# Two-layer cross-attention: the last 64 key columns computed by token beside the values, then turned by two transposes

## The reference, cut to what matters

```python
# layer 0: tokens 0..76 are text, 77..255 are image tokens
q = split_heads(x @ Wq.T); k = split_heads(text @ Wk.T); v = split_heads(text @ Wv.T)
k_ip = split_heads(ip @ Wk_ip.T); v_ip = split_heads(ip @ Wv_ip.T)
out = merge(attend(q, k, v)) + merge(attend(q, k_ip, v_ip))
x = out @ Wo.T + bo + x
# layer 1: tokens 0..251 are text, the last 4 image tokens
probs_t = softmax(q @ k_t.T / 4); text_out = probs_t @ v_t
qsem = l2norm(probs_t @ text); sem = qsem @ l2norm(ip).T
probs_ip = softmax(q @ k_ip.T / 4 + 0.5 * sem) * spatial_mask
x = merge(text_out + probs_ip @ v_ip) @ W_out + b_out + x
```

## Time and profile before

| what | value |
|---|---|
| median of three runs | 808.55 us |
| the profiled execution's own time | 811.3 us |
| its span, first to last instruction | 809.5 us |
| TensorE (PE) busy | 771.5 us, 95% |
| VectorE (DVE) busy | 562.1 us, 69% |
| ScalarE (ACT) busy | 426.0 us, 53% |
| GpSimd (POOL) busy | 402.2 us, 50% |
| mean granted TensorE clock | 0.992 |

### The profile page before, as it was taken

The page is one execution under the profiler, slowest core; times in us unless marked ns, Lnnn a source line. Parts: engine busy times, 40 slices in busy tenths (PEclk is TensorE's granted clock), DMA queues, the critical chain, the costliest instruction groups (busy, mean ns, idle before and its releaser), DMA issues.

```text
span 809.5 us, 17185 instructions
## 1 busy us (share of the span) xinstructions
PE 771.5 (95%) x6360; PEld 626.8 (77%) x6360; DVE 562.1 (69%) x1533; ACT 426.0 (53%) x913; POOL 402.2 (50%) x297
## 2 busy tenths in 40 slices
PE   5989899999999999999999999999999999988796
PEld 4888688888888878887877788788887887766474
DVE  4366465757576666758769778688697787686854
ACT  5234546463646474646465565555554655455551
POOL 5511222020202040405568877788769768779663
PEclk9999999999999999999999999999999999999998
DMA  7875835665647472736263355153172441400010
GB/s 245 212 210 157 212 112 135 197 159 158 162 126 184 126 202 76 211 99 170 70 150 94 90 143 151 45 160 112 49 190 69 111 126 62 113 1 26 12 33 17
DMA packets 103027, 100.67 MB, mean 124 GB/s; under 512 B 10264, under 2 KB 102176, under 8 KB 102944
## 3 DMA queue, kind: packets, MB, share of 16 engines
q1 hardware_dynamic: 101408, 98.26, 44.4%
q10 hardware_dynamic: 1536, 1.31, 0.6%
HBM read 61.65 MB, written 36.74 MB: 122 GB/s over the span
## 4 chain that ended last, share of the span: by engine, by line
PE 75%; DVE 9%; issue 4%; DMA 4%; POOL 3%; ACT 3%; SPq 1%; POOLq 0%; DVEq 0%; ACTq 0%
PE pB L384 22%; PE pB L500 12%; PE pB L463 8%; PE pB L486 8%; PE pB L584 5%; PE pPV L527 4%; PE pPV L522 4%; PE pPV L532 4%; PE pB L541 3%; PE pPV L518 3%; POOL Y L1306 2%; DVE m_sb L1061 2%; DVE m_sb L1059 2%; DMA QP<-mlo 1%; DMA Y<-in_Wk 1%
## 5 line engine op out<-in xcount | busy, mean ns | idle before, releaser
L1306 POOL TENSOR_TENSOR Y<-P,wv 128x512 f32<-128x512 f32 x120 | 156.2, 1318 | 107.8 <-ACT P L854 107.7
L1076 DVE TENSOR_TENSOR Y<-pB,Y 128x512 f32<-128x512 f32 x160 | 108.8, 686 | 70.0 <-PE pB L500 60.1
L463 PE MATMUL pB<-KP,QP 96*128 96x256 f32 x640 | 130.2, 288 | 2.7 <-DMA KP<-k0d 1.6
L1283 POOL TENSOR_TENSOR klo<-xin,khi 128x256 fp32r<-128x256 f32 x18 | 13.2, 756 | 228.8 <-ACT khi L765 228.8
L463 PEld LDWEIGHTS pB<-KP,QP 96*128 96x128 f32 x640 | 107.1, 192 | 16.5 <-issue 5.8
L1061 DVE TENSOR_REDUCE m_sb<-pB 128x2 f32<-128x504 f32 x160 | 108.0, 676 | 11.4 <-PE pB L463 9.7
L486 PE MATMUL pB<-QP,KP 100*128 100x512 f32 x320 | 108.3, 418 | 5.1 <-DMA QP<-mlo 4.4
L854 ACT ACTIVATE P<-pB 128x512 f32<-128x512 f32 x160 | 86.5, 597 | 42.0 <-PE pB L486 32.1
L854 ACT ACTIVATE P<-pB,ln 128x512 f32<-128x512 f32 x160 | 101.1, 691 | 0.0
L844 ACT ACTIVATE wv<-pB 128x512 fp32r<-128x512 f32 x120 | 66.8, 591 | 57.0 <-PE pB L486 55.7
L765 ACT ACTIVATE Vs<-pPV 128x512 f32<-128x512 f32 (+1 forms) x80 | 39.4, 492 | 101.8 <-PE pPV L522 68.4
(11 more groups left out here) (180 smaller groups left out, 1701.1 us busy)
## 6 DMA issues: line engine op xcount, KB each, us to landing
QP<-q0d SPq DMA_DIRECT2D x64, 192.0 KB, 4.1
KP<-k0d SPq DMA_DIRECT2D x64, 192.0 KB, 4.3
c_sb<-in_cT SPq DMA_DIRECT2D x16, 512.0 KB, 5.1
q0d<-qhi SPq DMA_DIRECT2D x32, 256.0 KB, 2.5
k0d<-khi SPq DMA_DIRECT2D x30, 256.0 KB, 2.5
q0d<-qlo SPq DMA_DIRECT2D x16, 256.0 KB, 2.8
k0d<-klo SPq DMA_DIRECT2D x15, 256.0 KB, 2.6
VB<-vipd SPq DMA_DIRECT2D x6, 640.0 KB, 4.0
```

The lines of the kernel that those rows point to most:

```text
L463: made = mm(bank[:, sc * S:sc * S + S], QP[i][0:KROWS, j, a, sc * 128:sc * 128 + 128], KP[i][0:KROWS, j, :], start=True, stop=True)
L1076: tt(Y[:, p, dst, :], bank_of["gp", q, dst][:, :], Y[:, p, dst, :], MUL).then_inc(dv_y, 1)
L1306: tt(Y[:, p, ch, :], P[:, p, ch, :], PH[q % HR][ch].bitcast(F32), SUB).then_inc(po_y, 1)
```

## The change

The last 64 key columns are no longer a job of matmuls with the weights stationary. Their weights (`wkz`) stand behind the value weights in one buffer (`wvk`), so that each matmul of V1 and V2 moves 384 columns instead of 320 and gives, by token, the image values and the last 64 image keys. ScalarE copies 128 columns of the result (the 64 keys with 64 value columns ahead of them) into `kz`; the job Kb is now two transposes of 128x128 of `kz`, after V2. Their result has the keys in partitions 64 to 127; the high part is written into `klo[64:128, 2]`, the low part into `klo[0:64, 2]`, a half buffer that the query and x tiles do not share. The third transpose of KT is made 128 wide, so that the text keys land in the same half.

The jobs' order changes with it (V1, V2 ahead of Kb; in layer 0 V0 between them, in layer 1 G0), and so do the pace table and the signals: the stores of `k0d` count on `l_k`, those of `k1d` on `l_kz`, and the load of the third key pack moves from step 9 of slot u to step 1 of slot u+1. In the prologue ScalarE and GpSimd split `wvi` ahead of `wv`, and ScalarE stores `k0d` after V1 and `k1d` after Kb.

```diff
-JOBS = (("Qa", "Qb", "Kt", "Ka", "Kb", "KT", "V0", "V1", "V2"),
-        ("Qa", "Qb", "Ka", "Kb", "V1", "V2", "G0", "G1"))
-SIZE = {"Qa": 16, "Qb": 8, "Kt": 12, "KT": 3, "Ka": 24, "Kb": 12, "V0": 12, "V1": 12, "V2": 12, "G0": 12, "G1": 12}
-PACE = ((14, 14, 13, 12, 12, 11, 10, 10, 9, 6), (13, 13, 12, 12, 12, 11, 11, 10, 8, 6))
-FIRST = (9, 9, 9, 9, 9, 9, 9, 9, 9, 30)
+JOBS = (("Qa", "Qb", "Kt", "Ka", "KT", "V1", "V2", "V0", "Kb"),
+        ("Qa", "Qb", "Ka", "V1", "V2", "G0", "Kb", "G1"))
+VALUES = ("V0", "V2")
+SIZE = {"Qa": 16, "Qb": 8, "Kt": 12, "KT": 3, "Ka": 24, "Kb": 2, "V0": 12, "V1": 12, "V2": 12, "G0": 12, "G1": 12}
+PACE = ((13, 12, 12, 11, 10, 10, 9, 9, 8, 7), (12, 12, 11, 11, 11, 10, 10, 9, 7, 5))
+FIRST = (8, 8, 8, 8, 8, 8, 8, 8, 8, 29)
...
-        wki = sb("wki", [128, 2, EC, C], F32R)
-        wvi = sb("wvi", [128, 2, EC, C], F32R)
+        wkm = sb("wkm", [128, 2, EC, 256], F32R)
+        wvk = sb("wvk", [128, 2, EC, C + 64], F32R)
+        wvi, wkz = wvk[:, :, :, 0:C], wvk[:, :, :, C:C + 64]
+        kz = sb("kz", [128, 2, 128])
...
+                    elif job == "Kb":
+                        pe.wait_ge(ac_bg, job_no(u, "V2"))
+                        for ch in range(2):
+                            made = nc.tensor.transpose(bank[:, 128 * ch:128 * ch + 128], kz[:, ch, :], ident[:, :])
...
+                        ts = slice(0, 128) if job == "V1" else slice(128, S)
+                        yield from chain(bank[:, 0:C + 64], [(c, v) for v, c in pairs512(wvk, slice(0, C + 64), ts)], pe_bg)
...
+                    if job != "V0":
+                        if u:
+                            ac.wait_ge(pe_bg, job_no(u - 1, "Kb"))
+                        copy(kz[:, int(job[1]) - 1, :], bank[:, C - 64:C + 64])
...
+                elif job == "Kb":
+                    ac.wait_ge(l_kz, 48 * u)
+                    if L == 0:
+                        copy(klo[64:128, 2, TXT0:S], bank[64:128, TXT0:S]).then_inc(ac_bg, 1)
...
-                            load_keys(sp, dma, u + 2, 2)
+                    if u >= 0 and u + 1 < U and j == 1:
+                        load_keys(sp, dma, u + 1, 2)
```

More of the change, by code:

```diff
@@ L417, in prepare @@
                     give(bank)
[L418 to L438, removed]
@@ L713, in store @@
                 else:
-                    dma(dram[1][0, z], tile[0:64, 2, :].bitcast(F32)).then_inc(signal, 16)
+                    rows = slice(64, 128) if tile is klo and not lows else slice(0, 64)
+                    dma(dram[1][0, z], tile[rows, 2, :].bitcast(F32)).then_inc(signal, 16)
         def store_queries(engine, dma, u, part):
@@ L719, in store_keys @@
         def store_keys(engine, dma, u, part):
-            job = "KT" if lay(u) == 0 else "Kb" if part else "Ka"
-            store(engine, dma, u, job, part, ((khi, 0, 0), (khi, 1, 0), (klo, 2, 1)), kd[u], l_k)
+            job = "Kb" if part else "Ka" if lay(u) else "KT"
+            hi = klo if part else khi
+            store(engine, dma, u, job, part, ((hi, 0, 0), (hi, 1, 0), (klo, 2, 1)), kd[u], l_kz if part else l_k)
         def head_rows(dram, m):
@@ L908, in scalar_program @@
             split_w(wk, sk0, (l_w["k0"], 16))
-            split_w(wki, ski0, (l_w["ki0"], 16))
+            split_keys(ski0, (l_w["ki0"], 16))
+            split_w(wvi, svi0, (l_w["vi0"], 16))
             split_w(wv, sv0, (l_w["v0"], 16))
-            split_w(wvi, svi0, (l_w["vi0"], 16))
             for job in JOBS[0]:
-                if job == "V0":
-                    for part in range(2):
-                        store_keys(ac, nc.scalar.dma_start, 0, part)
                 projection(0, job)
+                if job == "V1":
+                    store_keys(ac, nc.scalar.dma_start, 0, 0)
+            store_keys(ac, nc.scalar.dma_start, 0, 1)
             split_x(1)
@@ L1477, in sync_program @@
                             store_queries(sp, dma, a[0], a[1] == "Qb")
-                        elif what == "done" and a[1] in ("Ka", "Kb") and lay(a[0]) == 1:
-                            store_keys(sp, dma, a[0], a[1] == "Kb")
-                        elif what == "done" and a[1] == "KT":
-                            for part in range(2):
-                                store_keys(sp, dma, a[0], part)
+                        elif what == "done" and a[1] == ("Ka" if lay(a[0]) else "KT"):
+                            store_keys(sp, dma, a[0], 0)
+                        elif what == "done" and a[1] == "Kb":
+                            store_keys(sp, dma, a[0], 1)
                         elif what == "shift":
```

110 lines of the change are left out of this document (74 added, 36 removed).

## The result

The changed kernel takes **817.87 us** (median of 4 runs, 816.43 to 818.79) against 809.6 us for four runs of the kernel before on the same chip: a ratio of 1.0096, with an interval of 1.0073 to 1.012. It is slower by 1%. The forecast was 803.3 us, range 799.5 to 808.0. The profiled execution took 818.1 us, a span of 816.2, so 6.8 us more than the one of before where the sum gave 5.3 less: 12.1 us are to be explained.

A forecast was written before the change was run, and what follows sets the result against it. TensorE, busy 95% of the span, was taken to bound the kernel. Terms -3.9 - 0.5 - 1.2 + 0.35 gave -5.3 us, from the median of 808.55 to 803.3 us, range 799.5 to 808.0.

The forecast's parts named there:

- Kb's wait and its queue: TensorE's transposes wait for V2's copy, SP's k1d stores for a slot's end ahead of other transfers; priced at nothing.
- The clock: Slot 0's stretch at 1.2 GHz left as is; full clock, worth 1.8 us, put only into the range's lower end.
- Layer-1 units: Slots 6 to 13: fewer matmuls against wider value matmuls and two transposes, -0.49 us a slot, -3.9 us for eight.
- Layer-0 units: Slots 0 to 5: cheaper matmuls removed, same additions and a wider transpose, -0.09 us a slot, -0.5 us for six.
- The end of slot 0: First scores' 1.94 us wait for the maxima's rows shrinks as weight loads start earlier; gain 0 to 1.9, taken 1.2 us.
- The ends of slots 6 and 7: TensorE reaches first scores 0.35 us sooner; slot 6's wait for rows grows by that, slot 7's left to the range.
- ScalarE: Two more 128x128 copies a unit, 0.56 us a unit and 9 us in all, hidden by slack and costed at nothing.
- rival C: ScalarE becomes late, exposing kz and Kb copies: 0.92 us a slot, 12.9 us for 14, 816.2 us; chance 0.10.
- Rival B: TensorE's transposes cost their whole duration, 0.33 us more a unit, 4.6 us for 14 slots: 807.9 us; chance 0.17.
- Prologue and slot -1: Queries' copies start 1.3 us later, but a key load waits for fewer stores; taken 0, between -1.0 and +1.5 us.

The follow-up runs named there:

- Experiment 1: Changed kernel with only SP's k1d stores of layer-1 units moved behind step 8's loads: 811.41 us, ratio 1.0009 to the kernel before.
- experiment 2: Changed kernel with only the low part of layer 1's 64 key weight columns moved from VectorE to GpSimd: 814.6 us, ratio 1.0054.
- experiment 5: Kernel before with only layer 1's key weights split in two pieces (256 and 64 columns) on ScalarE and VectorE: 814.68 us, ratio 1.0045.
- Experiment 9: Changed kernel, k1d stores behind loads, 64-column low part on GpSimd, VY memset later, main key weights split earlier, second output weight in thirds: 804.9 us, ratio 0.9928.
- experiment 3: Changed kernel with both k1d stores behind step 8's loads and the 64 columns' low part on GpSimd: 808.15 us, ratio 0.9969.
- experiment 6: Changed kernel with ScalarE's kz copies issued twice in layer-1 units: 816.01 us, ratio 1.0074.
- experiment 10: Kernel before with only the split of layer 1's key weights moved from step 9 to step 7 of slot 5: 808.93 us, ratio 0.9968.

## Why the prediction was wrong

- **Kb's wait and its queue** is the first step that failed. It priced this at nothing: on SP the `k1d` stores "now wait for the end of a slot", and behind them stand the third query pack, the results and the residual. That is so in layer-0 units. In layer-1 units Kb is done in step 7, as the prediction's own rows of order for slot 10 show, and behind its stores stand all the loads of step 8, the first key pack of the next slot at their head. Experiment 1 prices it at 4.7 us of slot 7, a wait of 3.12 us and the slow clock behind it.
- **A term that was not there** is the second. The sum has no entry for the split of layer 1's key weights in two pieces at the end of slot 5, and gives no reason for leaving it out; in the prologue, with GpSimd idle, the second piece is cheap (0.42 us), and here it takes 2.45. It costs slot 6 4.4 us (experiment 2) and alone in the kernel before 2.5 us there and 0.45% in all (experiment 5).
- **The clock** was kept "as it is". Of the 9.5 us lost in slots 6 and 7, some 5 are clock: two waits of 1.6 us close together and one of 3.1 brought 1.2 GHz for 6.8 and 3.4 us. The prediction had seen such a stretch behind a wait, in slot 0, and had used it only as a possible gain.
- **Layer-1 units**, -0.49 us a slot: held in slots 8, 10, 11 and 12. Slots 10 to 12 went from 55.1 to 54.6, slot 8 from 54.4 to 53.9, and 13 value matmuls of 384 columns in slot -1 fill 50.77 to 53.02, 0.173 us each as forecast. TensorE's busy time fell by more, 0.6 us, and a new wait of 0.24 us for `ipS` (L1104) in each of these slots takes part of it. Slot 13 had a new wait of 0.5 us for a key pack. In slot 9 `P` comes 21.3 us into the slot in both kernels; TensorE is there earlier now and waits 1.55 us instead of 0.49. Experiment 9 brought `P` 0.5 us sooner by cutting ScalarE's weight split ahead of it, so it is that queue which sets its time. What delays the pack of slot 13 stays open.
- **Layer-0 units**, -0.09: not reached. Slots 2 to 5 rose by 0.2 to 0.5 us. The first maximum starts 0.2 to 0.5 us later in them; SP issues its key pack 2.3 us ahead of the slot (slot 4: 1.9) instead of 2.6, and in slot 4 the trace marks a wait of 0.26 us for it. The earlier trace rows could not show the pack as scarce because TensorE never waited for it. In experiment 9 they are at 37.4 to 37.5, so the matmuls saved here are worth nothing that shows.
- **The end of slot 0**, -1.2: the slot lost 1.4 (36.42 to 35.06), but the number was right by luck. The weight loads are issued 3.1 us earlier in the slot and the rows 0.7 us, and the wait went only from 1.94 to 1.58 us, because TensorE comes 1.0 us earlier in the slot too, which the sum did not have. In the other seven executions with the change this wait was between 0 and 1.5 us, in the three others without it 1.7 to 1.9, so on average the relief is larger than the term.
- **The ends of slots 6 and 7**, +0.35: did not show. Even in experiments 2 and 3, where slot 6 has its full clock, TensorE does not wait for the rows at its end; it waits 0.3 us for `Vs` instead. Slot 6 takes 40.1 and 40.3 us there, no less than before, since the wait for `Vs` near its start is 1.5 to 1.7 us instead of 0.97.
- **ScalarE** at nothing: held in the steady layer-1 slots (experiment 6), and with it the case against rival C. It is not shown for slots 6 and 9, where the waits for `Vs` and `P` grew by 0.6 and 1.1 us. Rival B fell too: the transposes show 272 ns each as their duration, but start 0.108 us apart, and slots 10 to 12 still saved all of the 0.5 us.
- **Prologue and slot -1**, 0: from TensorE's first matmul to the first scores pass 49.0 us instead of 48.9, and the slots begin 0.4 us earlier. Held.

The time came out near that of rival C, 816.2, but not for its reasons. With the two misfits mended, the ratio falls from 1.0096 to 0.9969, and 0.9969 of 808.55 is 806.0, inside the range that was given. That is no proof of the sum. In slots 1 to 13, where it had 4 us of gain, experiment 3 has 0.1: the 2.0 us of slots 8 and 10 to 12 went into slots 2 to 7 and 9. The gain that is left most likely comes from slot 0 and ahead of it, where the sum had 1.3 us.

## What to carry to other kernels

When work is reordered, follow each store and load of the moved job down its queue, for each kind of unit apart: which load stood behind it, and how long before its reader was it issued? A margin of 2.8 us, as here, is used up by one wait of 1.3 and three stores of 1.8, and no busy share shows it. And look at what happens once (the change of weights between layers), not only at the steady slots: here 9.5 of the 12.1 us that were missing lay in 2 of 17 slots. A wait of a few us in TensorE can be paid again in clock, as in slot 7. And measure the edits that mend a change in the kernel before as well: one of them alone was worth as much there (experiment 10).

## What the runs showed of the hardware

- VectorE's subtraction of 128x256 out of two SBUF operands took 0.42 us in the prologue, and 2.45 us where GpSimd's subtraction of 128x960 (2.92 us, from 291.56 on) had started first; it ended 0.28 us behind that one. The reductions, whose input is in PSUM, kept their 0.31 and 0.52 us beside GpSimd's work. The Trainium skill (SBUF — State Buffer, SBUF: two separate sides) says that of a VectorE instruction with two SBUF inputs and a GpSimd one that reads SBUF the second to start is blocked until the first ends. The traces agree: in experiment 5 VectorE's piece took 2.44 us and again ended 0.28 behind GpSimd's. And so one instruction cut in two pieces gives GpSimd the room to go in between.
- A wait of TensorE of 1.62 us, 1.4 us behind another of 1.61, was followed by 6.8 us at 1.2 GHz; one of 3.12 us by 3.4 us, and one of 3.87 us (experiment 2) by a slot at 0.92 of the clock. In the kernel before the wait of 0.97 us in slot 6 was followed by none. Nor was a single wait of 1.66 us in slot 6 of experiment 3 or one of 1.55 in slot 9 of the changed kernel. Wherever slot 6 had a slow stretch, two waits stood close together: 0.81 and 1.64 us in experiment 5, followed by 3.4 us, and 1.68 and 1.32 us in experiment 6, followed by 6.8.
- Mending one late place moves the next: in experiment 2 slot 7's wait grew from 3.12 to 3.87 us because TensorE arrived earlier.
